# Three PSUM slots that go round across groups, two more bursts of unread matrix multiplications, and another order of group 0's preparation, in a state-space tower

## The reference, cut to what matters

```python
A = -jnp.exp(A_log)
dbc = jnp.einsum('ble,ce->blc', x, W_dbc)
delta, Bm, Cm = jnp.split(dbc, [DT_RANK, DT_RANK + N_STATE], axis=-1)
delta = jax.nn.softplus(jnp.einsum('blr,er->ble', delta, W_dt) + b_dt)
dA = jnp.exp(delta[..., None] * A)
dBx = (delta * x)[..., None] * Bm[:, :, None, :]
...
y = jnp.einsum('blen,bln->ble', hs, Cm)      # hs: h = dA * h + dBx along l
return y + Dp * x
```

## Time and profile before

| | before |
|---|---|
| median of 3 runs (lowest, highest) | 6324.4 us (6324.39, 6329.62) |
| the profiled execution | 6317.07 us |
| its span, first to last instruction | 6315.2 us |
| mean granted clock of PE | 0.905 of 2.4 GHz |
| busy share PE, DVE, ACT, POOL | 79%, 95%, 79%, 93% |

### The profile page before, as it was taken

The page is one execution under the profiler, slowest core; times in us unless marked ns, Lnnn a source line. Parts: engine busy times, 40 slices in busy tenths (PEclk is TensorE's granted clock), DMA queues, the critical chain, the costliest instruction groups (busy, mean ns, idle before and its releaser), DMA issues.

```text
span 6315.2 us, 115575 instructions
## 1 busy us (share of the span) xinstructions
PE 4964.2 (79%) x35373; PEld 2008.5 (32%) x35373; DVE 6002.6 (95%) x4016; ACT 4959.9 (79%) x10247; POOL 5895.7 (93%) x996
## 2 busy tenths in 40 slices
PE   5777777777877777777787877778777778777789
PEld 2333333333333333333333333333333333333234
DVE  7999999999999999999999999999999999999965
ACT  5888888888888888888888877787887888887744
POOL 6999999999999999999999999999999999999933
PEclk7999999999899999999989888898998898998899
DMA  6887788787888888878888877788787787887810
GB/s 196 261 261 262 260 263 260 263 260 263 259 262 260 262 262 262 262 261 261 262 261 264 261 258 254 256 260 260 256 260 252 258 263 261 266 259 260 264 41 14
DMA packets 561605, 1561.17 MB, mean 247 GB/s; under 512 B 172113, under 2 KB 320530, under 8 KB 561298
## 3 DMA queue, kind: packets, MB, share of 16 engines
q1 hardware_dynamic: 561426, 1559.30, 76.0%
HBM read 1468.37 MB, written 90.59 MB: 247 GB/s over the span
## 4 chain that ended last, share of the span: by engine, by line
DVE 47%; issue 27%; PE 16%; POOL 4%; ACT 3%; DVEq 1%; DMA 1%; SPq 0%; ACTq 0%; POOLq 0%
DVE hT L923 46%; PE z_bank L418 5%; POOL u L1122 4%; PE decay L400 4%; ACT decay L706 2%; PE decay L540 2%; PE z_bank L428 1%; PE prep_bank L499 1%; DVEq L922 1%; PE decay L598 1%; DVE dx L934 1%; PE prep_bank L618 1%; PE prep_bank L444 1%; DMA u<-dx_rows 1%; PE decay L604 0%
## 5 line engine op out<-in xcount | busy, mean ns | idle before, releaser
L1122 POOL TENSOR_TENSOR u<-u,Bt 128x2976 f32<-128x2976 f32 x896 | 5788.6, 6495 | 219.0 <-DMA u<-dx_rows 217.3
L923 DVE TENSOR_TENSOR_SCAN hT<-decay,u 128x744 f32<-128x744 f32 x3584 | 5767.9, 1682 | 144.5 <-ACT decay L706 141.4
L706 ACT ACTIVATE decay<-decay,a_neg 128x371 f32<-128x371 f32 (+2 forms) x7168 | 3634.8, 555 | 641.1 <-PE decay L400 615.2
L400 PE MATMUL decay<-stk,spread 96*128 96x371 bf16 (+2 forms) x7168 | 1924.1, 356 | 1301.4 <-DVE hT L923 1206.3
L418 PE MATMUL z_bank<-hT,Cst 128*32 128x256 f32 x21472 | 1630.6, 427 | 0.0
L400 PEld LDWEIGHTS decay<-stk,spread 96*128 96x128 bf16 x7168 | 452.9, 101 | 2853.8 <-DVE hT L923 2616.7
L715 ACT COPY z_sb<-z_bank 128x512 f32<-128x512 f32 x1342 | 805.6, 600 | 375.3 <-PE z_bank L418 374.6
L418 PEld LDWEIGHTS z_bank<-hT,Cst 128*32 128x32 f32 x21472 | 601.4, 118 | 787.9 <-issue 545.0
L428 PE MATMUL z_bank<-stk,spread 96*128 96x372 bf16 x1341 | 325.5, 357 | 0.0
L499 PEld LDWEIGHTS prep_bank<-tmap,yT 64*128 64x128 f32 x1344 | 203.5, 215 | 134.5 <-issue 133.2
L499 PE MATMUL prep_bank<-tmap,yT 64*128 64x32 f32 (+3 forms) x1344 | 243.2, 306 | 0.7 <-DMA yT<-y_rows 0.7
(11 more groups left out here) (138 smaller groups left out, 2497.8 us busy)
## 6 DMA issues: line engine op xcount, KB each, us to landing
u<-dx_rows SPq DMA_DIRECT2D x3584, 372.0 KB, 4.1
delta_parts<-parts SPq DMA_DIRECT2D x112, 279.0 KB, 6.8
stk<-delta_parts SPq DMA_DIRECT2D x112, 279.0 KB, 5.3
y_rows<-z_sb SPq DMA_DIRECT2D x1792, 12.0 KB
yT<-y_rows SPq DMA_DIRECT2D x112, 192.0 KB, 4.4
dx_rows<-dx SPq DMA_DIRECT2D x112, 186.0 KB, 2.8
xT<-in_x SPq DMA_DIRECT2D x64, 186.0 KB, 4.3
xP<-in_x SPq DMA_DIRECT2D x64, 186.0 KB, 4.1
```

The source lines that it names most:

```text
L400: nc.tensor.matmul(slot[:, e, :, 1:], spread[0:PARTS * QR, TILES_G * q + er // TILES_G, :], src[:, er % TILES_G, :, 1:], start=True, stop= ...
L706: last = nc.scalar.activation(bank, bank, ACT.Exp, scale=a_neg[:, l, c:c + 1])
L923: nc.vector.tensor_tensor_scan(hT[q % 2][:, i * PAIR:(i + 1) * PAIR], pair_slot(p), u[c % RING][:, part * PAIR:(part + 1) * PAIR], 0.0, AL ...
L1122: tt(here, here, Bt[buf][:, :].unsqueeze(1).broadcast_to([P, 2 * HALVES * CHUNK, W0]), ALU.mult).then_inc(s_u, 1)
```

## The change

It has four parts. (1) Pair p of a group uses slot (turn + p) % 3, where turn is 32 times the group's number modulo 3. So the slots go round without a break, and every pair waits for the scan three pairs back. A body must know its turn when it is built, so the loop's body is now six groups (`ROUND_OF_GROUPS`): the layers have 2, 6 and 2 groups written out ahead of it, 10, 4 and 2 passes, and two groups behind it. As built, a loop's body of ACT has 352 instructions before and 1052 after, of DVE 162 and 482, of SP about 160 and 470, and of PE 498 and 1522 (there a multiplication and its load of weights count once); POOL's grows from 2 groups to 6 of eight products each. (2) `keep_busy` also at pair 25, and three unread multiplications into `prep_bank` at pair 31 (`keep_busy_in_prep`), behind the `post` of the group before. (3) The loads of the start in another order: `s5c`, `times`, `x` and three constants first, the other eight behind them, with a semaphore of their own each. (4) The tables' steps before or inside group 0's preparation, and the preparation of `a_neg`, `d_diag` and the cast of `spread` later in it.

```diff
-        def pair_slot(p):
-            return db[p % SLOTS][:, BANK - W0:BANK + W0]
+        def pair_slot(turn, p):
+            return db[(turn + p) % SLOTS][:, BANK - W0:BANK + W0]
...
+            def turn(l, g):
+                return PAIRS * (gbase[l] + g) % SLOTS
...
-                for g in range(2):
-                    body(g % 2, *group(l, g))
-                with eng.Fori(1, n // 2 - 1) as k:
-                    for half in range(2):
-                        body(half, *group(l, 2 * k + half))
+                first = 2 + (n - 4) % ROUND_OF_GROUPS
+                for g in range(first):
+                    body(g % 2, turn(l, g), *group(l, g))
+                with eng.Fori(0, (n - 2 - first) // ROUND_OF_GROUPS) as k:
+                    for g in range(ROUND_OF_GROUPS):
+                        body(g % 2, turn(l, first + g), *group(l, ROUND_OF_GROUPS * k + (first + g)))
...
-                if p >= SLOTS:
+                if p >= SLOTS or not known_below(n, 1):
                     pe.wait_ge(s_scan, PAIRS * n + p - SLOTS + 1)
-                elif not known_below(n, 1):
-                    pe.wait_ge(s_scan, PAIRS * n - (2, 1, 3)[p] + 1)
...
+            def keep_busy_in_prep(at, buf, before):
+                pe.wait_ge(s_post, G(before) + 1)
+                for _ in range(3):
+                    nc.tensor.matmul(prep[:, 0:W0], spread[0:PARTS * QR, 0, :], stk[buf][0:PARTS * QR, 0, :],
+                                     start=True, stop=True)
...
-                    if p in (8, 16, 24) or p == 1 and prev:
+                    if p in (8, 16, 24, 25) or p == 1 and prev:
...
+                    if prev and p == 31:
+                        keep_busy_in_prep(here, half, prev)
```

More of the change, by code:

```diff
@@ L21 @@
 EPT = D // TILES_G
+ROUND_OF_GROUPS = 6
 SLOTS = 3
@@ L246, in _ @@
         def _(sp):
[L247 to L255, removed]
             def load_x(at, buf):
@@ L321, in store_h, with body @@
                 sp.dma_start(hs[l][:, bass.ds(g * n, n)], y_out[:, 0:n]).then_inc(s_store, 16)
-            def body(half, here, prev, before, after):
+            def body(half, turn, here, prev, before, after):
                 for c in range(CHUNKS):
@@ L502, in to_channels, with body @@
                     last.then_inc(s_Y, 1)
-            def body(half, here, prev, before, after):
+            def body(half, turn, here, prev, before, after):
                 for p in range(PAIRS):
-                    spread_delta(here, half, p)
+                    spread_delta(here, half, turn, p)
                     q, i = divmod(p, TPAIRS)
@@ L786, in post, with body @@
                 nc.scalar.copy(y_out[:, 0:w], prep[:, 0:w]).then_inc(s_post, 1)
-            def body(half, here, prev, before, after):
+            def body(half, turn, here, prev, before, after):
                 for p in range(PAIRS):
-                    decay(here, p)
+                    decay(here, turn, p)
                     q, i = divmod(p, TPAIRS)
@@ L843, in _ @@
                 act_func_set_id=EXPS_ON_JOINT_TABLE))
+            high(first)
+            middle(first)
+            low(first)
+            act.wait_ge(s_const, 16 * N_CONST)
+            take_B(first, 0)
+            nc.scalar.activation(a_log[:, :, :], a_log[:, :, :], ACT.Exp).then_inc(s_aexp, 1)
+            act.wait_ge(s_aexp, 1)
+            nc.scalar.mul(a_neg[:, :, :], a_log[:, :, :], -1.0).then_inc(s_aneg, 1)
+            for l in range(LAYERS):
+                last = nc.scalar.mul(d_diag[:, l, :], d_diag[:, l, :], 0.5 if pair_mean[l] else 1.0)
+            last.then_inc(s_dout, 1)
+            take_C(first, 0, 0)
+            take_C(first, 0, 1)
+            act.wait_ge(s_aneg, 1)
             layer_bodies(act, body)
@@ L906, in _, with scan @@
                 nc.vector.memset(h[:, EPT * W0:EPT * W0 + TB], 0.0).then_inc(s_zero, 1)
-            dve.wait_ge(s_const, 16 * N_CONST)
-            for i in range(2):
-                src = hT[i][:, 0:EPT * P // 2].rearrange("p (r m) -> p r m", m=P)
-                last = nc.vector.tensor_copy(spread[:, i * EPT // 2:(i + 1) * EPT // 2, :], src)
-            last.then_inc(s_cast, 1)
-            dve.wait_ge(s_cast, 1)
-            def scan(at, p):
+            def scan(at, turn, p):
                 n = G(at)
@@ L934, in times_x, with body @@
                 tt(dx[:, :], prep[:, 0:W0], xT[buf][:, :], ALU.mult).then_inc(s_dx, 1)
-            def body(half, here, prev, before, after):
+            def body(half, turn, here, prev, before, after):
                 for p in range(PAIRS):
-                    scan(here, p)
+                    scan(here, turn, p)
                     if after and p == 9:
                         times_x(after, 1 - half)
-            times_x((0, 0), 0)
             dve.wait_ge(m_small, 16 * N_SMALL)
@@ L978, in _ @@
             ts(red, red, PI_LO, -PI_LO, ALU.min, ALU.max).then_inc(m_tab, 1)
+            dve.wait_ge(s_const, 16 * N_CONST)
+            for i in range(2):
+                src = hT[i][:, 0:EPT * P // 2].rearrange("p (r m) -> p r m", m=P)
+                last = nc.vector.tensor_copy(spread[:, i * EPT // 2:(i + 1) * EPT // 2, :], src)
+            last.then_inc(s_cast, 1)
+            dve.wait_ge(s_cast, 1)
+            times_x((0, 0), 0)
             dve.wait_ge(m_abig, 2)
```

59 lines of the change are left out of this document (28 added, 31 removed).

## The result

| | before | after |
|---|---|---|
| median of 4 runs | 6324.4 us (6320.9 to 6329.6) | 6181.8 us (6179.2 to 6189.5) |
| profiled execution, and its span | 6317.1, 6315.2 | 6180.2, 6178.2 |
| first scan starts, last scan ends | 67.4, 6019.5 | 33.6, 5881.3 |
| mean granted clock | 0.91 | 0.98 |

The ratio is 0.9776 with a 95% interval of 0.9759 to 0.9793: 143 us less, where 130 were forecast.

A forecast was written before the change was run, and what follows sets the result against it. POOL and DVE were taken as equally near their limit (51.63 and 51.64 us a group). -32 (start) - 165 (lost scan-phase time) + 33 (branches) + 34 (clock) = -130 us, giving 6194 us median, range 6150 to 6235.

The forecast's parts named there:

- The start: Ahead of the first scan: reordered loads and earlier tables bring it from 67.4 to 35.0 us, a gain of 32.4 us.
- The border: Between one group's last pairs and the next's first: new slots end the idle time there, within 165 us of lost time.
- one scan earlier, 1.7 us to spare: Pairs 0 and 1 wait for a scan 1.60 us earlier; 1.5 of 3.2 us is used, leaving 1.7.
- Gone where the clock stays up: At the group border: its loss was taken as gone wherever the granted clock stays up.
- The burst at 25: On PE at pair 25: keeps the clock up (45 us gained) or delays a late queue (25 us lost).
- The burst at 31: On PE at pair 31: three unread multiplications fill remaining idle time, occupy at most 1.6 us with spread, delay nothing.
- The clock: Allowance in the scan phase for clock falls: 34 us (0.3 us a group), from a stay of 0 to 70 us.
- The branches: At 13 branches back, all engines but POOL miss: 2.5 us each, 33 us, bounds 0 to 7.8 us each.
- slower: Rival: code fetched too late inside a pass, one 3.1 us stall in each of 112 groups, 6474 us; chance 0.04.
- The floor: Rival: bursts hold the clock, slack swallows the branches, POOL sets the pace; -196 us, 6128 us; chance 0.15.
- Half comes back: Rival: ACT and PE misses end to end, 13 x 7.8 = 101 us, clock falls cost 45; 6273 us; chance 0.15.
- Only the start: Rival: new slots do nothing because DMAs set POOL's broadcast waits; group stays 52.8 us; -32, 6292 us; chance 0.04.

The follow-up runs named there:

- start_only: Kernel after with the new slots, six-group loop and bursts at pairs 25 and 31 undone, leaving only the reordered loads and tables; 0.9954 to before.
- no25: Kernel after without the burst at pair 25; 0.9900 to before.
- straight: Kernel after with all 112 groups written out on every engine, no branch in the three layers; 0.9689 to before.

## Why the prediction was right

**The start: as forecast.** 33.8 us instead of 32.4; `start_only` has 29 (18 to 40).

**The border: gone, and for the reason given.** The step "one scan earlier, 1.7 us to spare" holds: pairs 1 to 5 lose 22 us after and 107 before, and 18 of the 22 stand behind branches. "Gone where the clock stays up" holds as well, and says too little. Even the old slots lose next to nothing where the clock stays up, and the new ones lose next to nothing where it is down, unless a burst stands at pair 31 (second table). What the prediction called the second effect of the idle time, the fall to the lower level, is the larger one: nearly the whole 1.1 us a group needs it.

**The burst at 25: the gain, not the loss, and larger than I had bounded it.** I put 45 us behind it, from 27 waits of before; before loses 46.8 ahead of pairs 28 to 31. But `no25` loses 80.3 there, and after 3.7: the burst removes 77 us, as the ratio says (78). The price of a group in which the clock falls was right (1.2 us before, 1.3 in `no25`); their number was not, 39 before and 61 in `no25`. Whether the slots or the longer loop made it 61 no run tells apart. **The burst at 31** delays nothing where the clock is up, as forecast; where it is down it costs 0.39 us (`no25`), which the prediction ruled out; and it gains no measurable time either.

**The clock: 34 us allowed, at most 10 met.** `straight` loses 10.4 us in 112 groups, 0.1 us a group instead of 0.3, although the clock is at the lower level for 175 us. The prediction's floor (5787, from 1.601 us a scan) is 11 us above the table's (1.598); against its own, `straight` with 5786.5 loses nothing and after 61.

**The branches: 33 us allowed, 61 met.** This is the term that was mis-sized, together with the clock's. 13 waits of 2.7 to 4.1 us stand in DVE's timeline, 43.5 us in all (9 in layer 1, 3 in layer 2, 1 in layer 3), 3.35 us each where 2.5 were taken. The other third follows: PE restarts at the lower level and DVE waits again for one or two of the next three pairs, 0.39 and 1.04 us at 455 and 459. The wait of before was also less even than "as long at 10 places": 1.2 to 2.1 us. The two errors, 28 too little here and 34 too much at the clock by the prediction's own floor, nearly cancel. That is luck: with the clock's term right and this one as it was, the forecast would have been 6160. The forecast of 6194 against 6182 (6187 against 6180 for the profiled execution) is better than its terms. The range is not quite their sum either: clock 0 to 50 and branches 10 to 60 around 6194 give 6137 to 6237, not 6150 to 6235, and the 61 us lie just outside "10 to 60".

The Trainium skill, "Advanced Engine Details and Errata", section ISA Cache, gives sizes: two lines of 256 instructions on an engine, four times the memory on TensorE. The trace agrees so far as instruction packets rose from 49 to 324 on one queue and from 130 to 364 on the other when the bodies grew to three times their length. The section has no duration; the rows give it. The case "slower" took four lines per pass and feared each; `straight` uses no instruction twice and loses 10.4 us, so only the fetch behind a jump is waited for.

**The rivals.** *The floor* (6128): after doesn't reach it, `straight` does, with 0.9689 x 6324.4 = 6128 us and its last scan at 5820.2, where POOL's floor had been put at 5823. What speaks against it in after is the branch and not, as I wrote, a fall at pair 24. *Half comes back* (6273): the misses stand side by side. Its 7.8 us a branch doesn't follow from its rows, where a double wait of 3.9 and PE's 3.14 add up to 7.0, which would give 6263. A second wait does follow in layer 2 (3.30 and 2.00 us at 4005.7 and 4009.4), but no branch costs 7.8 us or 7.0; the dearest group behind one loses 5.8. *Only the start* (6292): the DMAs' waits were an echo, as above. *Slower*: no stall in mid-group.

**What would show it.** First scan 33.6; groups of 51.6; POOL's wait under 100; waits of 2.7 to 4.1 at 13 branches, with instruction packets in all three loops: all found.

## What to carry to other kernels

Repairs of one engine's lateness change each other's worth: both bursts are worth 0.39% in the old order and 1.17% in the new (0.9893 against 0.9776), so a trace of before bounds a part only for the state that it shows. A body that no longer stays on its engine pays at the jump alone, and pays on several engines at once: writing out a part of them freed about a third of the 61 us, writing out all of them freed all. A rarer jump helps nearly in proportion. The version to keep is the one with all groups written out, 0.9689 (0.9673 to 0.9705) to before and 0.9% under the kernel after.

## What I had not expected of the hardware

- Code without jumps costs next to nothing here even when none of it is used twice: 10.4 us lost over 112 groups, against 4.7 us for each jump back of the kernel after.
- Each engine misses by itself: DVE stands for 2.86 us, ACT for 4.1 and PE for 3.75 to 5.46 in the rows above. All at the same moment cost 4.7 us a jump, and with a part of them freed still 3.0 to 3.4 (49.3 - 10.4 to 54.7 - 10.4 us, by 13).
- Three unread multiplications at pair 25 raise the mean clock from 0.92 to 0.98. Three more at pair 31 change it by 0.01 and the time by nothing measurable, though the time at the lower level is 396 us without and 229 with them.
- The kernel without a jump and with every burst still ran at 0.935 while the old slots left PE idle for 2.32 us at a border; with the slots going round it is 0.98. So less idle time at one place raised the mean clock about as much as three multiplications at another. How the chip weighs the two isn't settled by these runs.
- The same late slot costs 1.2 to 1.3 us where the clock falls at the border and 0.0 to 0.2 where it stays up; the new slot costs nothing at either level as long as nothing is added at pair 31.
